# Windowed cross attention with a routed low-rank FFN: score products on four 32x32 parts of the array instead of two 64x64 parts

## The reference, cut to what matters

```python
# attention, batch by batch: x, cond are 128 x 1024, 8 heads of 16 channels, window of 16 keys
x = layernorm(x)                       # over the 1024 positions
q, k, v = Wq @ x + bq, Wk @ cond + bk, Wv @ cond + bv
dots = einsum('bhdt,bhdtw->bhtw', qh, k_win) * scale      # query t sees keys t-8 .. t+7
attn = softmax(dots); out = einsum('bhtw,bhdtw->bhdt', attn, v_win)
x = x + Wo @ out + bo
# FFN: 8 experts of rank 64, the two best of each row are mixed
xn = layernorm(x)
probs = softmax(xn @ gate_w.T); weights, sel = top_k(probs, 2); weights /= sum(weights)
x = x + sum_e w_full[:, e] * (xn @ A[e].T @ B[e].T)
```

## Time and profile before

| | |
|---|---|
| median of 3 runs | 1184.99 us |
| the profiled execution | 1181.87 us, span of its trace 1180.1 us |
| TensorE matmul busy | 1118.5 us (95%), 16384 records |
| TensorE weight load busy | 965.0 us (82%), 16384 records |
| VectorE busy | 904.6 us (77%) |
| ScalarE, GpSimd busy | 391.8 us, 408.9 us |
| granted TensorE clock, mean | 0.99 |

### The profile page before, as it was taken

One profiled execution on the slowest core, in us unless ns is written; L12 is line 12 of the kernel. 1 busy time (PEld: TensorE's weight loads), 2 busy tenths in 40 slices (PEclk: granted clock), 3 DMA queues, 4 the chain that ended last, 5 costly groups with the idle time before them and its releaser, 6 DMA issues.

```text
span 1180.1 us, 38884 instructions
## 1 busy us (share of the span) xinstructions
PE 1118.5 (95%) x16384; PEld 965.0 (82%) x16384; DVE 904.6 (77%) x2021; ACT 391.8 (33%) x553; POOL 408.9 (35%) x302
## 2 busy tenths in 40 slices
PE   1677999999999999999999999999999999999987
PEld 1566888888888888888888888888888888888875
DVE  3576787877778787787878787888778787877763
ACT  3323433333333333333332333323333333233221
POOL 4443333333323334333333433333343233333210
PEclk9988999999999999999999999999999999999999
DMA  7344334455443355443345543434554433454200
GB/s 226 68 90 90 93 86 79 91 109 104 89 96 81 72 108 109 94 96 93 77 81 110 109 89 95 94 70 92 110 108 90 95 86 75 97 110 91 56 37 36
DMA packets 423345, 108.68 MB, mean 92 GB/s; under 512 B 405904, under 2 KB 406032, under 8 KB 423056
## 3 DMA queue, kind: packets, MB, share of 16 engines
q1 hardware_dynamic: 423184, 106.11, 41.6%
HBM read 55.22 MB, written 16.78 MB: 61 GB/s over the span
## 4 chain that ended last, share of the span: by engine, by line
PE 83%; DVE 4%; issue 4%; POOL 4%; SPq 3%; ACT 1%; DMA 1%; DVEq 0%; POOLq 0%; ACTq 0%
PE bank_a L314 29%; PE bank_b L342 19%; PE bank_c L314 15%; PE bank_b L363 14%; PE bank_a L372 4%; PE bank_b L332 2%; SPq L240 2%; DMA raw<-x 1%; DVE stats L616 1%; POOL prob L842 1%; SPq L249 1%; POOL attn_split L863 1%; POOL src_split L857 1%; POOL src_split L848 1%; ACT k_sb L591 1%
## 5 line engine op out<-in xcount | busy, mean ns | idle before, releaser
L342 PEld LDWEIGHTS bank_b<-k_sb,q_diag 64*64 64x64 f32 x8192 | 249.8, 135 | 29.6 <-issue 29.6
L342 PE MATMUL bank_b<-k_sb,q_diag 64*64 64x32 f32 x8192 | 264.0, 220 | 0.0
L842 POOL TENSOR_TENSOR prob<-prob,row_inv 128x512 f32<-128x512 f32 x128 | 134.2, 1048 | 262.1 <-DVE row_inv L705 262.1
L314 PE MATMUL bank_a<-down_split,mid_split 128*128 128x264 f32 (+1 forms) x1536 | 216.8, 291 | 1.8 <-DVE mid_split L748 1.8
L363 PEld LDWEIGHTS bank_b<-prob_t,v_diag 64*64 64x64 f32 x4608 | 187.6, 133 | 25.8 <-issue 16.4
L314 PE MATMUL bank_c<-src_split,w_split 128*128 128x512 f32 x576 | 161.9, 418 | 49.0 <-ACT k_sb L591 22.8
L363 PE MATMUL bank_b<-prob_t,v_diag 64*64 64x96 f32 (+2 forms) x4608 | 201.7, 238 | 0.9 <-DMA v_diag<-v_t 0.9
L314 PEld LDWEIGHTS bank_a<-down_split,mid_split 128*128 128x128 f32 x1536 | 191.4, 188 | 7.1 <-ACT mid_split L545 1.9
L314 PE MATMUL bank_a<-up_split,ht_split 128*128 128x512 f32 x768 | 188.7, 395 | 1.5 <-DVE ht_split L787 1.5
L528 ACT ACTIVATE prob<-prob 128x512 f32<-128x512 f32 x128 | 80.8, 631 | 296.5 <-DVE prob L693 294.7
L314 PEld LDWEIGHTS bank_c<-src_split,w_split 128*128 128x128 f32 x576 | 107.5, 196 | 81.0 <-ACT k_sb L591 32.4
(11 more groups left out here) (68 smaller groups left out, 1100.8 us busy)
## 6 DMA issues: line engine op xcount, KB each, us to landing
v_diag<-v_t SPq DMA_DIRECT2D x128, 132.0 KB, 5.4
raw<-x SPq DMA_DIRECT2D x32, 512.0 KB, 4.4
raw<-ctx SPq DMA_DIRECT2D x32, 512.0 KB, 5.8
q_diag<-q_xn SPq DMA_DIRECT2D x256, 64.0 KB, 3.6
resid_pair<-x SPq DMA_DIRECT2D x32, 512.0 KB, 3.2
out<-resid_pair SPq DMA_DIRECT2D x32, 512.0 KB, 2.6
v_diag<-up_w SPq DMA_DIRECT2D x1, 2048.0 KB, 10.6
prob_t<-down_w SPq DMA_DIRECT2D x1, 780.0 KB, 6.2
```

The costliest lines, as they stand in the source:

```text
L314: return nc.tensor.matmul(dst, st[:, s, st_cols], mv[:, m, mv_cols], start=start and n == 0, stop=stop and n == 2)
L342: last = nc.tensor.matmul(bank_b[m % 2][rows, t * KT:(t + 1) * KT], q_diag[rows, cur.parity, n, :], keys[rows, n * QT:n * QT + KT], start= ...
L842: nc.gpsimd.tensor_tensor(weights_of(m), weights_of(m), row_inv[:, cols].unsqueeze(2).broadcast_to([P, CT, KT]), ALU.mult).then_inc(prob_d ...
```

## The change

The two calls for a query tile become four, each on 32 rows with 32 stationary columns, so on four 32x32 parts on the diagonal of the array. Two heads share a part. The number of moving columns stays 32. `q_diag` becomes half as wide (32 columns for each tile), since a row needs room for two heads' positions only; the DMAs write the same bytes at another offset. The mask matmul and the weighted chunks are untouched.

```diff
-        q_diag = sb("q_diag", [P, 2, TILES, HALF_P])
+        q_diag = sb("q_diag", [P, 2, TILES, PW])
...
-                    at = HD * h % HALF_P
+                    at = HD * h % PW
                     sp.dma_start(q_diag[rows, ahead.parity, :, at:at + QT],
                                  tiles[rows]).then_inc(q_placed, 16)
...
-                    for z in range(HALVES):
-                        rows = slice(z * HALF_P, (z + 1) * HALF_P)
+                    for g in range(PAIRS):
+                        rows = slice(PW * g, PW * (g + 1))
                         last = nc.tensor.matmul(bank_b[m % 2][rows, t * KT:(t + 1) * KT],
                                                 q_diag[rows, cur.parity, n, :],
                                                 keys[rows, n * QT:n * QT + KT], start=False,
```

## The result

The changed kernel takes 1277.2 us (median of 4 runs, 1269.25 to 1294.08) against 1185.8 us before (median of four runs now, the three named above and one more of 1186.56): a ratio of 1.0754, 95% interval 1.0698 to 1.0809. The ratio leaves out the slow run of 1294.08 us, which lies over 1.5% above the fastest. Forecast was 1164 us, range 1142 to 1212. The time is outside the range and on the other side of no change.

What follows compares the result with a forecast made beforehand. Two level chains, TensorE's work and a ring through VectorE, GpSimd, a DMA and ScalarE, were taken to bound the kernel; savings of 17 us (steady steps), 3 (end) and 0.7 (start) make 21, giving 1164 us, range 1142 to 1212.

Steps and rivals of the forecast that it cites:

- The chunk on the array: Score chunk on TensorE: four parts work side by side, 34 ns for four records, 1.09 us a chunk, 0.75 less.
- the rival built on a price per record: Score records: each keeps its price on four parts, 1424 us at 29.2 ns or 1359 at 25 ns; chance 0.15.
- The steady step: Steady steps: TensorE's work falls from 34.64 to about 31.6 us, the saving mostly turns into waiting; 28 x 0.6 = 17 us.
- the ring: Chain through VectorE, GpSimd, one DMA and ScalarE, as long as TensorE's 34.64 us step, without score chunks; it stays.
- its 0.6 us: Steady step: the saving of 0.6 us in each of 28 steps, 17 us; bounds 0 and 84.
- wait for `h_sb`: Sign of being right: TensorE waits for `h_sb` (L676) and `k_sb` (L591) some 2 to 3 us a step.
- My sum of 21 us: Whole kernel: 17 us in steady steps, 3 at the end and 0.7 at the start.
- my two terms of 0.3 us: Steady step: 0.3 us from steps free of waits for TensorE, 0.3 from an earlier store, residual load and `ctx`.
- the step from 757.88 us: Step where `ctx` lands sooner: L759 starts 9.37 us in, not 11.03; VectorE gives 1.66 us back waiting for TensorE.
- The rival with the clock: TensorE's clock falls behind the wait before the transposes: about 1184 us if every step, 1174 if half; chance 0.12.
- go in pairs: Score chunk: only two parts work at a time, 2.05 us a chunk, 0.21 more, 1212 us; chance 0.08.

Runs made afterwards that it cites:

- e4: Changed kernel with q and k rounded to bf16 for the scores, 128 instructions a chunk instead of 256; 1161.5 us.
- e2: Changed kernel with only eight of each chunk's sixteen tiles on four parts, the other eight on two; 1168.2 us.
- e8: Changed kernel with twelve of each chunk's sixteen tiles on four parts, the other four on two; 1174.0 us.
- e11: The kernel with twelve of sixteen tiles on four parts, its TensorE loop moved to place 77 of a 256-instruction block; 1175.6 us.
- e10: The kernel with eight of sixteen tiles on four parts, its TensorE loop moved to place 200 of a 256-instruction block; 1183.7 us.

## Why the prediction was wrong

**The chunk on the array: right.** I said 1.09 us from its first record to the next product instead of 1.84 to 1.98. Undisturbed chunks take 1.21 to 1.37; their best row is 1.29 us long and so 1.10 us from first record to last (8.7 ns a record, where 34 ns for four had been taken, 8.5). The Trainium skill, "TensorE: Matmul & The Clock Gate", in the part on "56ns, not 53.3ns", has a floor of about 25 ns from start to start; the records on four parts were far below it, at 9 ns in e4, so the rival built on a price per record was rightly put low, and it was not what made the kernel slower.

**The steady step: this is where the prediction failed.** It said "TensorE's own step falls from 34.64 to about 34.64 - 4 x 0.75 = 31.6 us" and that the ring would bound the step at 34. This counted what the array does and never what it takes to bring it its instructions. With the rows of after, a step is: 34.6 less 4 x 0.77 (1.98 before, 1.21 now) = 31.5 us; breaks before score, weighted and down records, (117.5 + 6.8 + 2.2)/32 = 4.0; the lower clock, by an estimate (0.990 - 0.945) x 1276.6 / 32 = 1.8 (57 us in all; the rows say nearly the same, 908 - 855 = 54 us more busy time in the matmuls other than the scores). Together 37.3 against 38.2 measured; 0.9 is not accounted for. So TensorE stayed the bound, 3.6 us a step above before, and 28 steps make 101 us; the span grew by 96.5.

**The ring: right as the next bound, its 0.6 us not secured.** Where the supply hardly breaks, the period is 34.0 (e4), 34.1 (e2), 34.3 (e8), 34.5 (e11) and 34.5 us (e10), against 34.6 before and the forecast's 34.0, with its wait for `h_sb` of 2 to 3 us in e4 alone. And e4 also moves less data (its q placement is half as large), so its period can't be put to the ring alone. My sum of 21 us is near what e2 (17 us) and e4 (24) gain; but e11 and e10, with 9 and 1, show that the 0.6 us a step are not to be had at each placement, and no run tells my two terms of 0.3 us apart. In the reading of the step from 757.88 us one row was misread: of the two waits in which VectorE gives time back, the one of 0.49 us ends with ScalarE, not TensorE, and the two make 1.77 us, not 1.66.

**The rival with the clock: right in kind, wrong in weight.** The clock did fall behind waits, and it cost nothing that shows where the ring bounds (e4), but some 54 to 57 us, by the working above, where TensorE does. It fell there behind the breaks and not behind the wait for `h_sb` that I had named. In the forecast it was to cost only the gain.

**The chances.** Slower had 0.25: 0.23 on records that cost more at the array or go in pairs, 0.02 on the clock. The case that came wasn't among them, and the range ended at 1212. A row of the profile could have told me before the run: `q8 instruction` with 152 packets stood in the profile, and the change added 16384 instructions to 38884 on all engines, in bursts. The Trainium skill, "Runtime: NRT & Kernel Launch", section "Instruction fetch mechanics", says that code comes in blocks of 16 KiB, 256 instructions, with two lines on the engine (though it also gives 128 KiB for TensorE, eight such blocks), and that crossing a block is "mostly hidden". The block size agrees with 64 packets for 16384 instructions here and with breaks that lie multiples of 256 apart; "mostly hidden" held before (no issue idle in the score records) and did not hold at 256 instructions in about 1.2 us.

## What to carry to other kernels

When a change makes an engine's instructions smaller and more, compare the rate at which it uses them up, in its densest stretch, with the spacing of instruction packets in the trace (for 256 here, behind a break, 3.4 us at the least and 4.1 in the median), not only the time that they take on the array. Idle time with reason "issue" in the middle of a run of like instructions, at the same instruction in every pass of a loop, is a want of code; moving the loop by some places in the code is the test that changes nothing else, and may be most of the cure. Stay below the rate where it begins: here 192 to 224 instructions in 1.5 to 1.8 us hardly broke, at two placements each, and 256 in 1.2 us did.

## What the runs showed that I had not expected

- Where a loop lies in the code moved the same kernel by 86 us, 1179.4 to 1265.6, and a kernel with hardly any breaks by 15 (1168.2 to 1183.7), the latter unexplained.
- Records on four parts of the array start 8.7 to 9 ns apart (e4: 64 in 0.58 us).
- A break ends 2.2 to 2.8 us after its packet starts, and the packets themselves take about 1 us each (1.1% of 16 engines' span of 1276.6 us, over 216).
- Cutting a chunk of tiled records in four pieces added 0.4 us a chunk to its busy time (50.7 us in 128).
